# A routed-expert layer's last stage: weighted sums moved from VectorE and ScalarE to TensorE, and one shared-expert chunk moved behind the expert tiles

## What is computed

```python
tg, ti = jax.lax.top_k(softmax(relu(xf @ Wr1 + br1) @ Wr2 + br2), 2)
tg = jax.nn.softmax(tg / 2, axis=-1)
out = silu(xf @ Ws1 + bs1) @ Ws2 + bs2          # shared expert, every token
for e in range(8):                              # routed experts
    h = silu(xf @ We1[e] + be1[e]) @ We2[e] + be2[e]
    out = out + jnp.sum(tg * (ti == e), axis=-1)[:, None] * h
x = x + gb * out                                # gb: one gate row per sequence
```

## Time and profile before

| what | us |
|---|---|
| device time, 3 runs: median (lowest to highest) | 914.73 (913.86 to 918.37) |
| the profiled execution, device time | 918.26 |
| its span (first to last instruction) | 916.4 |
| so around the span | 1.9 |

### The profile page before, as it was taken

One profiled execution on the slowest core, in us unless ns is written; L12 is line 12 of the kernel. 1 busy time (PEld: TensorE's weight loads), 2 busy tenths in 40 slices (PEclk: granted clock), 3 DMA queues, 4 the chain that ended last, 5 costly groups with the idle time before them and its releaser, 6 DMA issues.

```text
span 916.4 us, 22613 instructions
## 1 busy us (share of the span) xinstructions
PE 803.8 (88%) x8710; PEld 553.1 (60%) x8710; DVE 576.4 (63%) x1587; ACT 387.7 (42%) x765; POOL 271.2 (30%) x268
## 2 busy tenths in 40 slices
PE   4765989999989989999999999988999799999940
PEld 3452556666645646656656566555567688889940
DVE  8476776666689988677687786876556222222218
ACT  3583221222256315625346254465654343444423
POOL 2580000000176510012020120214776244544430
PEclk9796999999979959999999999999999799999985
DMA  6700131427205952134241342222324167777746
GB/s 199 297 1 1 36 138 34 167 93 245 80 1 151 316 152 59 29 101 93 50 106 27 101 96 49 60 41 59 79 72 140 51 187 209 212 216 218 229 125 212
DMA packets 107827, 108.37 MB, mean 118 GB/s; under 512 B 48892, under 2 KB 93644, under 8 KB 106796
## 3 DMA queue, kind: packets, MB, share of 16 engines
q1 hardware_dynamic: 103196, 97.82, 37.1%
q0 software_dynamic: 4544, 9.35, 2.9%
HBM read 82.15 MB, written 44.78 MB: 139 GB/s over the span
## 4 chain that ended last, share of the span: by engine, by line
PE 57%; DVE 19%; DMA 7%; issue 6%; ACT 5%; POOL 4%; SPq 2%; POOLq 0%; DVEq 0%; ACTq 0%
PE bank L1975 7%; PE bank L2204 6%; PE bank L2214 5%; PE bank L1801 5%; PE bank L1812 5%; PE bank L1813 5%; DVE sb_arena L1400 5%; PE bank L1867 4%; PE bank L1915 4%; DMA expert_results<-sb_arena 4%; PE bank L1893 2%; PE bank L2123 2%; PE bank L1842 2%; PE bank L2133 2%; DVE sb_ST L1089 1%
## 5 line engine op out<-in xcount | busy, mean ns | idle before, releaser
L1400 DVE TRANSPOSE_TENSOR_REDUCE sb_arena<-bank 128x16 f32<-128x512 f32 x192 | 120.3, 685 | 24.9 <-PE bank L1915 23.6
L967 ACT ACTIVATE sb_arena<-bank 128x512 f32<-128x512 f32 x192 | 99.2, 602 | 41.1 <-PE bank L1915 41.1
L1055 ACT ACTIVATE sb_arena<-bank,sb_arena 128x256 f32<-128x256 f32 x156 | 65.3, 471 | 99.0 <-PE bank L2204 98.3
L791 POOL DMA_INDIRECT expert_results<-sb_arena x78 | 74.7, 957 | 93.5 <-DVE sb_arena L1668 81.0
L891 ACT ACTIVATE sb_arena<-bank 128x512 f32<-128x512 f32 x64 | 38.1, 597 | 143.5 <-PE bank L1813 143.5
L1801 PEld LDWEIGHTS bank<-sb_arena 128*128 128x128 f32 x512 | 68.2, 196 | 41.9 <-issue 25.7
L2204 PE MATMUL bank<-sb_arena 128*128 128x256 f32 x312 | 79.1, 398 | 5.0 <-DVE sb_arena L1664 4.8
L1801 PE MATMUL bank<-sb_arena 128*128 128x128 f32 x512 | 70.5, 281 | 10.0 <-DVE sb_arena L1227 10.0
L2214 PE MATMUL bank<-sb_arena 128*128 128x128 f32 x624 | 76.2, 276 | 0.0
L1227 DVE TENSOR_TENSOR sb_arena<-sb_arena,bank 128x512 f32<-128x512 f32 x64 | 43.6, 684 | 49.7 <-ACT sb_arena L891 49.5
L2214 PEld LDWEIGHTS bank<-sb_arena 128*128 128x128 f32 x624 | 73.2, 193 | 0.1
(11 more groups left out here) (265 smaller groups left out, 1371.3 us busy)
## 6 DMA issues: line engine op xcount, KB each, us to landing
sb_arena<-in_w SPq DMA_DIRECT2D x39, 578.0 KB, 4.1
dispatched_rows<-in_padding SPq DMA_DIRECT2D x8, 2064.0 KB, 9.6
sb_arena<-dispatched_rows SPq DMA_DIRECT2D x39, 129.0 KB, 2.2
sb_arena<-q_parts SPq DMA_DIRECT2D x8, 512.0 KB, 5.7
sb_arena<-k_parts SPq DMA_DIRECT2D x8, 512.0 KB, 7.0
context_rel<-sb_arena SPq DMA_DIRECT2D x256, 8.0 KB
sb_arena<-expert_results SPq DMA_DIRECT2D x16, 256.0 KB, 6.1
q_parts<-sb_arena SPq DMA_DIRECT2D x24, 128.0 KB, 3.3
```

Source lines behind the costliest of these rows:

```text
L791: nc.gpsimd.indirect_dma_start(yD[:, :], bass.IndirectOffsetOnAxis(ap=rid[:, k, r:r + 1], axis=0), YS[:, k, r, :], None).then_inc(s_yo[k], 16)
L967: nc.scalar.activation(dst, src, ACT.Exp).then_inc(s_ex, 1)
L1400: v.tensor_reduce(dst.rearrange("p h b -> p (h b)"), bank[r % RING][:, :].rearrange("p (b c) -> p b c", c=32), AX, ALU.max, apply_transpos ...
```

## The change

VectorE and ScalarE no longer form the weighted sums at the end. In the tile loop, after each `results`, VectorE makes two 128 by 128 diagonal matrices for one group of 128 tokens (identity times the group's weights, `diagonal(T)`), 64 matrices in all. At the end TensorE multiplies each group's `YG[0]` and `YG[1]` by its diagonal matrices and adds both in PSUM (`weighted_sum`), eight matmuls per chunk, a bank per chunk; VectorE runs `add_gated` from PSUM. The shared expert's last chunk is taken out from ahead of the tiles; its hidden layer, its bias (a product of a row of ones with the bias row) and its down product run behind the last tile, and stay in the bank in which the chunk's weighted sum is then added (`last_shared`). The waits for `s_sdn` and `s_res` go from 8 to 7.

```diff
--- before.py
+++ after.py
@@ -259,6 +259,10 @@
         R = Region(early)
         ROWS = [v.rearrange("p (t n) -> p t n", t=NT) for v in (rows0, R.take(NT * RW))]
         YG = [v.rearrange("p t n -> p (t n)")[:, 0:NT * D].rearrange("p (t n) -> p t n", t=NT) for v in ROWS]
+
+
+        diagonals = [arena[:, at:at + NT * P].rearrange("p (t n) -> p t n", t=NT) for at in (TOK, R.at)]
+        assert TOK + NT * P <= pt_at and R.at + NT * P <= attn_end
 
 
         R = Region(pt_at)
@@ -400,10 +404,14 @@
         s_yo = [sem(f"s_yo{k}") for k in range(UT)]
         s_yl = [sem(f"s_yl{c}") for c in range(NC)]
         s_turn = sem("s_turn")
-        s_y1 = sem("s_y1")
+        s_dg = sem("s_dg")
+        s_sum = sem("s_sum")
         s_fin = sem("s_fin")
 
         block = ctx.enter_context(nc.Block())
+
+        def sum_bank(c):
+            return bank[4 if c == NC - 1 else c if c < 4 else c + 1]
 
         def early_bank(n, c):
             return bank[(0 if n else 6) + c % 2]
@@ -625,7 +633,7 @@
             sp.wait_ge(s_rl, 4 * NP)
             for k in range(UT):
                 load_weights(k, k)
-            sp.wait_ge(s_sdn, NC)
+            sp.wait_ge(s_sdn, NC - 1)
             for k in range(2):
                 sp.wait_ge(s_disp[k], 16 * NT)
             for k in range(UT):
@@ -1042,7 +1050,7 @@
             relu(7)
             rows_out(7)
             shares(3)
-            for c in range(4, NC):
+            for c in range(4, NC - 1):
                 shared_hidden(c)
             act.wait_ge(s_lg, GROUPS + 2)
             nc.scalar.activation(b_w2[:, :], b_m2[:, :], ACT.Exp).then_inc(s_el, 1)
@@ -1062,13 +1070,11 @@
                     hidden(i * UT + k, k)
             for k in range(LAST):
                 hidden(FULL * UT + k, k)
-            act.wait_ge(s_lg, GROUPS + 3)
-            for c in range(NC):
-                act.wait_ge(s_yl[c], 32)
-                for t in range(TPC):
-                    T = c * TPC + t
-                    ins = nc.scalar.activation(YG[0][:, T, :], YG[0][:, T, :], ACT.Copy, scale=b_w1[:, T:T + 1])
-                ins.then_inc(s_y1, 1)
+            act.wait_ge(s_dn[1], NG)
+            for b in range(KB1):
+                act.wait_ge(s_sup, (NC - 1) * KB1 + b + 1)
+                nc.scalar.activation(HM1[:, 0, b, :], bank[b][:, :], ACT.Silu, bias=W1S[:, 2 * I1 + b:2 * I1 + b + 1]
+                                     ).then_inc(s_sact, 1)
 
 
         @block.vector
@@ -1668,6 +1674,13 @@
                 v.tensor_tensor(YS[:, k, :, :], bank[6 + k % 2][:, 0:GT].rearrange("p (r n) -> p r n", r=2),
                                 W1[:, k, OB:OB + D].unsqueeze(1).to_broadcast([P, 2, D]), ALU.add).then_inc(s_ys, 1)
 
+            def diagonal(T):
+                for weights, matrix in zip((b_w1, b_w2), diagonals):
+                    ins = v.tensor_tensor(matrix[:, bass.ds(T, 1), :], ident[:, :].unsqueeze(1),
+                                          weights[:, bass.ds(T, 1)].unsqueeze(2).to_broadcast([P, 1, P]), ALU.mult)
+                ins.then_inc(s_dg, 1)
+
+            assert UT * (FULL - 1) == NT
             step = [0, 0]
             tile_in(0, 0)
             for j in range(UT):
@@ -1679,6 +1692,7 @@
                     step[:] = (i, 0) if k < UT - 1 else (i + 1, 0)
                     tile_in(i * UT + k + 1, (k + 1) % UT)
                     results(i * UT + k - 1, (k - 1) % UT)
+                    diagonal(i * UT - UT + k)
             last = FULL * UT
             for k in range(LAST):
                 if k < LAST - 1:
@@ -1686,15 +1700,10 @@
                 results(last + k - 1, (k - 1) % UT)
             results(NG - 1, LAST - 1)
 
-            dve.wait_ge(s_res, NC)
+            dve.wait_ge(s_res, NC - 1)
             for c in range(NC):
-                dve.wait_ge(s_y1, c + 1)
-                dve.wait_ge(s_yl[c], 32)
-                for T in range(c * TPC, (c + 1) * TPC):
-                    ins = v.scalar_tensor_tensor(out=YG[0][:, T, :], in0=YG[1][:, T, :], scalar=b_w2[:, T:T + 1],
-                                                 in1=YG[0][:, T, :], op0=ALU.mult, op1=ALU.add)
-                link(ins)
-                add_gated(c, YG[0][:, c * TPC:(c + 1) * TPC, :].rearrange("p (b t) f -> p b t f", b=2), 1, s_fin)
+                dve.wait_ge(s_sum, c + 1)
+                add_gated(c, sum_bank(c)[:, :].rearrange("p (b t f) -> p b t f", b=2, t=2), 1, s_fin)
 
 
         @block.tensor
@@ -2184,9 +2193,7 @@
             shared_down(4)
             shared_up(6)
             shared_down(5)
-            shared_up(7)
             shared_down(6)
-            shared_down(7)
 
             def transpose_tile(j, k, arrived):
                 pe.wait_ge(s_xr[k], arrived)
@@ -2216,7 +2223,7 @@
                                  skip_group_check=True)
                 ins.then_inc(s_dn[1], 1)
 
-            pe.wait_ge(s_res, NC)
+            pe.wait_ge(s_res, NC - 1)
             transpose_tile(0, 0, 16)
             for j in range(UT):
                 up_tile(j, j, 16)
@@ -2235,6 +2242,33 @@
                     transpose_tile(last + k + 1, k + 1, 16 * (FULL + 1))
                 down_tile(last + k - 1, (k - 1) % UT)
             down_tile(NG - 1, LAST - 1)
+
+            def last_shared(c):
+                for b in range(KB1):
+                    mm(bank[b][:, :], W1S[:, b * P:(b + 1) * P], chunk(hT, c), start=True, stop=True).then_inc(s_sup, 1)
+                for t in range(TPC):
+                    mm(sum_bank(c)[:, t * D:(t + 1) * D], ones[0:1, :], W1S[0:1, OB:OB + D], start=(t == 0), stop=False,
+                       skip_group_check=True)
+                pe.wait_ge(s_sact, (c + 1) * KB1)
+                for t in range(TPC):
+                    for b in range(KB1):
+                        mm(sum_bank(c)[:, t * D:(t + 1) * D], HM1[:, 0, b, t * P:(t + 1) * P],
+                           W1S[:, I1 + b * D:I1 + (b + 1) * D], start=False, stop=False, skip_group_check=True)
+
+            def weighted_sum(c):
+                pe.wait_ge(s_yl[c], 32)
+                for t in range(TPC):
+                    T = c * TPC + t
+                    for k in range(2):
+                        ins = mm(sum_bank(c)[:, t * D:(t + 1) * D], diagonals[k][:, T, :], YG[k][:, T, :],
+                                 start=(k == 0 and c < NC - 1), stop=(k == 1), skip_group_check=True)
+                ins.then_inc(s_sum, 1)
+
+            last_shared(NC - 1)
+            pe.wait_ge(s_ys, NG)
+            pe.wait_ge(s_dg, NT)
+            for c in range(NC):
+                weighted_sum(c)
 
 
 _SHAPE = (16, 256, 128)
```

## The result

| what | before | after |
|---|---|---|
| median of 20 runs each, in turn on one chip (us) | 916.93 (911.84 to 921.47) | 911.22 (905.18 to 913.95) |
| the profiled execution, device time (us) | 918.26 | 908.76 |
| its span (us) | 916.4 | 906.9 |

The ratio is 0.9932, with an interval of 0.9918 to 0.9945: of 916.93 us that is 6.2 us gained, 5.0 to 7.5. The forecast was 5.2 us.

What follows compares the result with a forecast made beforehand. TensorE was taken to bound the tile loop nearly everywhere, VectorE the final sums from chunk 1 on. Front, diagonals and moved chunk were priced 0, the sums gained 5.2 us: 914.73 - 5.2 = 909.5 us, range 907.2 to 915.0.

Steps and rivals of the forecast that it cites:

- The tail: Sums behind the last tile: TensorE's 1.79 us a chunk replaces VectorE's 2.67; gain 5.2 us.
- The moved chunk at the end: Behind the last tile, TensorE's last shared chunk runs beside the scatter and loads of results: price 0, 1.1 us of cover.
- The front: Ahead of the tiles, removing the last shared chunk: sum taken as 0, bounds -0.4 to +1.0 us.
- The low clock at the start of the tiles: First transposes meet 1.2 GHz, as already before: +0.2 us; a clock returning a little later gives the +1.0 bound.
- the moved chunk is covered where it stands: Ahead of the tiles, TensorE's shared expert ends 0.94 us before the last scatter's landing.
- The diagonals: Tile loop: 0.57 us a step, 18 us of VectorE in all, inside its waits for landings; price 0.
- A: Rival: clock falls in the tail's gaps; gain 0 (914.7), or 1.7 us lost (911.2); chance 0.16.
- B: Rival: diagonals meet the loop's scatters, 0.49 us more each; gain 2.7 us, 912.0; chance 0.10.
- C: Rival: low clock holds for the whole tail, 3.58 us a chunk; 7.3 us slower, 922.0; chance 0.06.
- D: Rival: loads bound the sums in the tail, so they get no shorter; gain under 3 us, 912; chance 0.06.

Runs made afterwards that it cites:

- e1b: e1 with 40 products that nobody reads ahead of the sums, in place of TensorE's idle time; 966.21 us, ratio 0.996 to the kernel before.
- e7: Changed kernel plus a 512-column VectorE product with two SBUF operands after each step's diagonals; 913.04 us against 918.19 for the kernel before, ratio 0.9928.
- e8: Changed kernel with GpSimd's 64 scatters of dispatched rows held back until all tokens are routed; 976.61 us, ratio 1.0634 to the kernel before.
- e9: Changed kernel with the shared expert of chunk 6 left out altogether; 912.91 us, ratio 0.9939 to the kernel before.
- e1: Changed kernel with the shared expert's last chunk back ahead of the tiles (sums on TensorE alone); 966.89 us, ratio 0.9957 to the kernel before.
- e0: The changed kernel run again, on a chip where the kernel before took 971.58 us; 961.7 us, ratio 0.9899.
- e4: Changed kernel with one pair of diagonals, made ahead of the first tile and used for all tokens; 963.34 us, ratio 0.9905 to the kernel before.
- e3: Changed kernel with every diagonal pair made twice, four products a step; 965.5 us, ratio 0.9937 to the kernel before.
- e5: Changed kernel with 30 products that nobody reads ahead of the first tile, to raise the clock; 967.79 us, ratio 0.994 to the kernel before.

## Why the prediction was right

**The two numbers.** The median was forecast at 909.5 us in a range from 907.2 to 915.0, and came out at 911.22. Of the 1.7 us between, 2.2 are the kernel before, whose median was 914.73 in three runs and 916.93 in twenty; the gain was 1.0 larger than the 5.2 forecast, which itself lies within the interval.

**The tail, the whole of the forecast.** From the first load's issue the forecast had 911.2 - 887.16 = 24.0 us; the profile has 24.1, and the experiments keep it at 23.8 to 24.4 wherever the sums are on TensorE, but for e1b. Its steps, one by one: a chunk's sum 1.79 forecast, 1.82 measured; the gaps ahead of chunks 0 and 1 1.2 and 1.5 forecast, 1.11 and 1.29 measured; VectorE waits for TensorE in each chunk, as foreseen; last sum to the end of the span 1.5 + 2.7 forecast, 906.9 - 902.68 = 4.2 measured.

**The moved chunk at the end.** Forecast 8.1 to 8.3 us of TensorE with 1.1 to spare; measured 885.48 - 877.03 = 8.45, with 1.11 to spare ahead of chunk 0. The bias products took 1.15 us and the down products 3.84, each 0.2 over my price.

**The front: the term with a wrong size.** I had named that L1166 might leave the last scatter (0 to 0.4 us), and that the first transposes might meet a low clock (+0.2), and took the sum as 0. Measured is a gap of 5.45 for 6.02, and 5.4 to 5.5 in e7, e8 and e9. 0.49 of the 0.57 is the scatter, 0.96 for 1.45; the transposes did take 0.66, but behind the point that the gap ends at. The sum should have been 5.2 + 0.6 = 5.8, nearer to the 6.2 measured. The rest, 0.4 us, is within the interval. A second thing came out otherwise there. The low clock at the start of the tiles was forecast to last as before or longer. In both profiles the granted clock is 0.50 for 10.24 us, but before that stretch starts at 722.45, behind the first transpose, and after it starts at 716.97, ahead of it, in the longer idle time that the moved chunk leaves; so it reaches 10.5 us into the tiles before and 4.5 after. In e7 and e9, from another chip without the 50 us, it reaches 4.3 us in (e7 has 3.4 us more of it later). That can shorten the loop, by an amount that the medians leave little room for.

**The front on other chips.** "So the moved chunk is covered where it stands" holds where the scatter lands last. The cover was 0.94 us, by my own rows. Where TensorE is late it is gone, and the chunk in front costs 3.5 us (e1 against e0, by the gaps of their profiles).

**The diagonals.** Price 0 held as far as these runs can tell (1 or 2 us stay possible): 0.283 us each for the 0.285 of the nearest row, no charge for the address from a register, and VectorE's wait for landings paid for them (e4, e0, e3). Between before and after that wait fell by 10 us, not by the 18 forecast; between e4 and e0 by 17. I had them end 0.6 us behind the results, of 0.79 allowed; measured 0.41 of 0.80.

**The rivals.** A was not seen in the changed kernel (PEclk 1.00), but once in e1b, at 1.6 us, behind gaps about twice as long. B's collision is real: e7 brought it about at 0.08 us a scatter and lost nothing; at 0.49 us it was not seen in the loop. C did not come, and e1 speaks against it, in one execution: met at 0.50, the clock was back after 3.7 us of dense sums. D did not come: after chunk 1 no gap, 112 rows in 12.77 us.

**What the profile can't give.** That the profiled spans differ by 9.5 us was no sign of a larger gain: 5 of it is a loop of 154.3 us for 159.2. Fewer us at 0.50 (4.5 for 10.2) go with it; by e5's measure 5.7 us less of low clock are 2 us or so (an estimate from one pair of profiles), and the other 3 stay open: e9, with 4.3 us at 0.50, had a loop of 156.8. With 5.1 us for the tail and 0.6 for the gap, the interval of 5.0 to 7.5 leaves 1.8 us at most for the loop.

## What to carry to other kernels

Work may be added to the busiest engine if it goes into a stretch where that engine is idle: price the stretch, not the share of busy time. Where work waits on two things, note by how much the first beats the second (here 0.94 us): that is how far a price of zero reaches, and on another chip it may not. Before a difference of two profiled spans is taken for a gain, cut both into the stretches that the change touches and those that it doesn't.

## What was not expected of the hardware

**The same program takes 50 us more on some chips.** The kernel before has a median of 971.58, 971.91 and 967.75 us on three chips, and 918.19 on the fourth. The loop and the tail are alike, and the first scatter starts as early (632.3 us in e0, 632.4 in the changed kernel's first profile); the time goes between about 640 and 770 us, while GpSimd scatters and the other engines route tokens and run the shared expert. e0 there, in windows, and its timeline:

```profile
702.00:712.00 10.00, 4.70 (x20) 2.44 (x18) 0.56 (x5) 0.30 (x1) 7.56 (x9) 0.85 0.16 53
...
752.00:762.00 10.00, 3.27 (x8) 2.20 (x8) 0.00 (x0) 0.94 (x1) 5.74 (x6) 0.57 0.45 150
```

```profile
757.21 0.37 PE L2142 MATMUL bank<-sb_arena 128*128 128x128 f32 x1 [1.57 <-issue]
758.48 0.96 POOL L791 DMA_INDIRECT dispatched_rows<-sb_arena  x1 [0.30 <-issue]
...
762.32 0.69 DVE L1584 TENSOR_TENSOR sb_arena<-bank,sb_arena 128x512 f32<-128x512 f32 x1 [16.33 <-remote]
```

The changed kernel on the other chip, also with GpSimd busy scattering:

```profile
700.00:710.00 10.00, 10.00 (x69) 8.09 (x69) 5.21 (x16) 5.54 (x7) 7.56 (x9) 1.00 0.68 218
```

GpSimd does as much in both, 7.56 us and 9 instructions in 10 us, but in e0 TensorE does 20 rows where the other does 69, and it waits between them for nothing that the profile knows ("issue"). That speaks against a wait for data, and the scatters are what runs beside it; but no cause is shown. The fetching of instructions may be thought of, and nothing in the trace speaks for it: between 640 and 770 us the two instruction queues moved 6 packets in e0 and 10 in the changed kernel's first profile. e8 was to test the scatters and met a chip without the loss.

**The low clock's price is less than the lost cycles.** 10.2 us at half the clock are 5.1 us of full-speed work lost; the loop was about 4 us longer for them (e5 against e0, one profile each, with the table's other rows in line). That other waits took up the rest is likely and not shown.
